# The routed part of a second FFN, computed for all tokens by every expert or for sorted blocks of 128 pairs

## The chip, the core and the metric

One Trainium2 chip, one of its cores. The program is written engine by engine: TensorE (PE, matrix products and transposes into PSUM), VectorE (DVE), ScalarE (ACT), GpSimd (POOL) and SyncE (SP, which issues the transfers), each with its own list of instructions, tied together by semaphores. The metric is the time of one execution in microseconds, the median of several. PSUM has 8 banks of 128 x 512 floats.

## The reference, cut to what matters

All is float32; 4 batches of 256 tokens, width 256, so 1024 tokens, computed in two halves of 512.

```python
x = x + ssm(ctx, layernorm(x))      # scan over 256 steps, 256 channels, 16 states
    # delta = softplus(dt_proj_w @ dt_lo + dt_proj_b);  state = state*exp(delta*A) + delta*u*B
x = x + ffn0(layernorm(x))          # 32 experts of 96 hidden units, top 8
x = x + cross_attention(layernorm(x), ctx)   # 16 heads of 128, 8 key heads
x = x + ffn1(layernorm(x)):
    shared   = silu(x @ wg_s) * (x @ wu_s) @ wd_s * 0.1          # 256 hidden units
    affinity = sigmoid(x @ centroids.T)                          # 16 experts
    top_idx  = top_k(affinity + gate_bias, 2)
    weights  = affinity[top_idx] / (sum of the two + 1e-9)
    for e in range(16):                                          # 128 hidden units each
        routed = routed + mask[:, e] * (silu(x @ wg[e]) * (x @ wu[e]) @ wd[e])
    return shared + routed
```

Each token uses 2 of the 16 experts; for the others its weight is zero.

## The kernel before, in words

A **half** is 512 tokens, 4 chunks of 128. Stages follow each other: the scan of half 0 (DVE: `scan_state` and `scan_read`, one pair for each of 16 states), the scan of half 1 interleaved with the first units of FFN 0, the rest of FFN 0, attention (64 head units, one for each half, head and batch), and FFN 1.

A **unit** of an FFN is 128 hidden units of weights times one half. `gate_up(u)` makes x @ gate and x @ up into two banks, ACT applies Silu (`activate_gate`), DVE multiplies by the up side and by the row of routing weights (`multiply_hidden`), and `down(u - 2)` adds the product with the down weights into two banks that hold the sum over all experts. Every unit multiplies all 512 tokens of its half, whether they chose the expert or not, and tokens of no weight are multiplied by zero. FFN 1 has 36 units: 2 of shared weights and 16 experts, for each half.

Nearly all products are made as **three products of a split** (`product3`): each operand is stored as a rounded high part and a rest, and hi x hi, hi x rest and rest x hi are added in PSUM. A unit is thus 12 + 6 = 18 instructions of 512 columns. The splitting costs too: ACT rounds each weight piece (`round_weights`), POOL subtracts (`rest_weights`), and the hidden values go through ACT and DVE (`round_hidden`, `rest_hidden`). The first 12 units of FFN 0 work on whole float32 operands instead (`gate_up_whole`, `down_whole`), where one product is recorded as two matmul instructions.

The order is written out by hand: each engine's list has loops over units or head units, and the steps between stages are numbered `transition(k, step)`: k = 6 and 7 lead from attention to FFN 1 for half 0 and 1, k = 8 and 9 from FFN 1 to the output. Steps 0 to 3 copy and turn the sum, add it to `x_tok` and find the variance, 4 normalises, 5 and 6 turn x for the products, 7 and 8 make the router's logits, 9 and 10 pick the two experts (`rank_experts`, `choose_two`, a row of small dependent DVE instructions), 11 turns the weights into rows. SP loads weights with `fetch`, broadcasts routing rows from a scratch in DRAM with `load_routes`, and stores the output pair by pair (`store_out`). An engine's list is executed in order: an instruction that waits holds up all behind it.

POOL's part in attention is `normalise(i)` for each head unit: it scales the probabilities by their inverse sums, and PE turns them two head units later (`turn_probs`, line 695). In the scan of half 0, ACT makes delta as Softplus with a bias (`activate_delta`), the decays as Exp (`scan_decay`), and the gate z (`normalise_z`, `activate_z`); the fold of the attention weights (`fold_turn`, `fold_multiply`) is laid between the scan's steps on PE and ACT.

## Time and profile before

| what | value |
|---|---|
| median of 3 runs | 744.71 us (744.0 to 747.23) |
| profiled execution, its own time | 747.59 us |
| profiled execution, span from first to last instruction | 745.9 us |
| PE busy | 682.9 us, 92% |
| DVE, ACT, POOL busy | 68%, 57%, 38% |
| mean granted clock of TensorE | 0.973 of full |
| moved by DMA | 88.1 MB |

By the timeline the stages are: scan of half 0 to about 90 us, scan of half 1 beside FFN 0 to 195 us, the rest of FFN 0 to about 354 us, attention to about 583 us, FFN 1 to the end. A busy share of PE is a sum over matrix products whose recorded durations overlap; the cost of one in a row of many is read from the distance between starts.

### The profile page before, as it was taken

How to read it: one execution, taken by the hardware profiler on the slowest of the kernel's cores; microseconds unless marked ns; L12 is line 12 of the kernel's file. 1: busy time of each engine (PE TensorE's matmuls, PEld its weight loads, DVE VectorE, ACT ScalarE, POOL GpSimd, SP SyncE). 2: the span in 40 equal slices, each digit the busy share in tenths (PEclk: the TensorE clock that was granted, in tenths of full speed). 3: DMA queues.
4: the chain of work that ended last, by engine and by line, in shares of the span. 5: the costliest groups of instructions: out<-in, count | busy, mean ns of one | idle time of the engine just before them, and what ended most of it. 6: DMA issues, size and time to landing. Idle time of an engine off the chain costs nothing.

```text
span 745.9 us, 10129 instructions
## 1 busy us (share of the span) xinstructions
PE 682.9 (92%) x3450; PEld 531.9 (71%) x3450; DVE 504.8 (68%) x990; ACT 423.7 (57%) x835; POOL 286.8 (38%) x266
## 2 busy tenths in 40 slices
PE   6476679999989999999899999997999899999997
PEld 1164445555767888887789999876997777888885
DVE  5789999999656655564766667766665566545444
ACT  5776746462265455454777777676876454343442
POOL 1456410002333334453555646444656243122131
PEclk9589987999999999999999999999999999999999
DMA  7359945676442644442110101100121235333240
GB/s 243 132 189 286 326 150 168 209 206 162 126 148 89 184 130 154 145 156 67 53 34 29 57 30 43 44 29 15 59 65 57 86 127 168 103 108 107 89 127 28
DMA packets 43666, 88.14 MB, mean 118 GB/s; under 512 B 6072, under 2 KB 8384, under 8 KB 43616
## 3 DMA queue, kind: packets, MB, share of 16 engines
q1 hardware_dynamic: 43616, 87.51, 37.5%
q8 instruction: 27, 0.44, 0.2%
q14 instruction: 23, 0.19, 0.1%
HBM read 81.92 MB, written 5.57 MB: 117 GB/s over the span
## 4 chain that ended last, share of the span: by engine, by line
PE 72%; DVE 13%; ACT 10%; issue 3%; POOL 0%; DMA 0%; SPq 0%; DVEq 0%; ACTq 0%
PE bank L91 19%; PE bank L92 19%; PE bank L93 19%; PE bank L503 5%; DVE state L1178 4%; PE bank L514 3%; PE bank L695 3%; ACT probs L1053 2%; ACT bank L813 2%; PE bank L422 2%; DVE scores L1459 1%; DVE head_out_lo L1103 1%; PE bank L410 1%; DVE x_tok L1202 1%; ACT head_out_hi L778 1%
## 5 line engine op out<-in xcount | busy, mean ns | idle before, releaser
L1532 POOL TENSOR_TENSOR w_lo<-w_raw,w_hi 128x768 fp32r<-128x768 f32 (+1 forms) x94 | 156.8, 1668 | 287.9 <-ACT w_hi L778 286.7
L91 PE MATMUL bank<-xt_hi,w_hi 128*128 128x512 f32 x352 | 140.7, 400 | 1.3 <-DVE hidden_lo L1103 1.3
L93 PE MATMUL bank<-xt_hi,w_lo 128*128 128x512 f32 x352 | 139.5, 396 | 0.0
L92 PE MATMUL bank<-xt_lo,w_hi 128*128 128x512 f32 x352 | 138.9, 395 | 0.0
L778 ACT ACTIVATE w_hi<-w_raw 128x768 fp32r<-128x768 f32 (+1 forms) x94 | 72.4, 770 | 103.0 <-PE bank L93 91.7
L1103 DVE TENSOR_TENSOR hidden_lo<-bank,hidden_hi 128x512 fp32r<-128x512 f32 x72 | 49.6, 690 | 67.6 <-ACT hidden_hi L778 67.6
L1342 DVE TENSOR_TENSOR bank<-gated,bank 128x512 f32<-128x512 f32 x68 | 47.2, 694 | 56.1 <-PE bank L93 52.7
L1053 ACT ACTIVATE probs<-scores,row_min 128x256 f32<-128x256 f32 x128 | 63.9, 501 | 25.7 <-DVE row_min L1459 25.5
L91 PEld LDWEIGHTS bank<-xt_hi,w_hi 128*128 128x128 f32 x352 | 66.2, 188 | 16.2 <-DVE hidden_lo L1103 2.1
L93 PEld LDWEIGHTS bank<-xt_hi,w_lo 128*128 128x128 f32 x352 | 66.1, 188 | 15.9
L921 ACT ACTIVATE gated<-bank 128x512 f32<-128x512 f32 x84 | 50.2, 597 | 46.0 <-PE bank L503 30.2
L92 PEld LDWEIGHTS bank<-xt_lo,w_hi 128*128 128x128 f32 x352 | 66.1, 188 | 13.7
L778 ACT ACTIVATE hidden_hi<-bank 128x512 fp32r<-128x512 f32 x72 | 42.5, 590 | 51.6 <-DVE bank L1345 50.1
L1603 POOL TENSOR_TENSOR probs<-probs,row_scale 128x512 f32<-128x512 f32 x64 | 66.7, 1042 | 5.0
L1459 DVE CUSTOM_DVE_ANT_0 scores<-bank,mask_bias 128x256 f32<-128x256 f32 x128 | 48.8, 418 | 13.8 <-PE bank L93 13.7
L91 PE MATMUL bank<-hidden_hi,w_hi 128*128 128x512 f32 x144 | 56.9, 395 | 0.8 <-DVE hidden_lo L1103 0.8
L92 PE MATMUL bank<-hidden_lo,w_hi 128*128 128x512 f32 x144 | 57.1, 396 | 0.0
L93 PE MATMUL bank<-hidden_hi,w_lo 128*128 128x512 f32 x144 | 56.1, 390 | 0.0
L1103 DVE TENSOR_TENSOR probs_t_lo<-bank,probs_t_hi 128x512 fp32r<-128x512 f32 x64 | 44.1, 688 | 15.4 <-ACT probs_t_hi L778 15.3
L778 ACT ACTIVATE probs_t_hi<-bank 128x512 fp32r<-128x512 f32 x64 | 38.2, 596 | 28.5 <-PE bank L695 28.1
L422 PEld LDWEIGHTS bank<-identity,read_out 128*128 128x128 f32 x272 | 31.9, 146 | 30.6 <-DVE read_out L1188 20.5
L422 PE MATMUL bank<-identity,read_out 128*128 128x128 f32 x272 | 37.2, 284 | 14.4 <-DVE read_out L1188 14.4
(173 smaller groups left out, 1451.0 us busy)
## 6 DMA issues: line engine op xcount, KB each, us to landing
w_raw<-in_ffn_w SPq DMA_DIRECT2D x62, 384.0 KB, 3.2
b_rows<-bc_scratch SPq DMA_DIRECT2D x32, 256.0 KB, 4.4
c_rows<-bc_scratch SPq DMA_DIRECT2D x32, 256.0 KB, 3.7
w_raw<-fold_scratch SPq DMA_DIRECT2D x32, 256.0 KB, 2.6
route_bc<-route_scratch SPq DMA_DIRECT2D x32, 256.0 KB, 3.6
route_bc<-route_scratch SPq DMA_DIRECT2D x31, 192.0 KB, 3.4
w_whole<-in_ffn_w SPq DMA_DIRECT2D x12, 384.0 KB, 4.8
fold_scratch<-fold_sb SPq DMA_DIRECT2D x8, 512.0 KB, 4.8
```

Source lines behind the costliest of these rows:

```text
L91: e.matmul(out, w_hi, m_hi, start=first, stop=False)
L92: e.matmul(out, w_hi, m_lo, start=False, stop=False)
L93: return e.matmul(out, w_lo, m_hi, start=False, stop=last)
L422: last = e.matmul(ps[:, l * DI + c * P:l * DI + (c + 1) * P], tile[:, c, t:t + P], identity[:, :], is_transpose=True, start=n < 0 and l + ...
L778: e.activation(out, source, ACT.Copy).then_inc(sem(name), 1)
L921: e.activation(gated[u % 2][:, :], bank[4 + 2 * (u % 2)][:, :], ACT.Silu).then_inc(sem("silu"), 1)
L1053: last = e.activation(probs[i % 3][:, r, :], scores_sb[i % 2][:, r, :], ACT.Exp, scale=-1.0, bias=row_min[i % 2][:, r:r + 1], accum_out=ro ...
L1103: e.tensor_tensor(out_lo, source, out_hi.bitcast(F32), ALU.subtract).then_inc(sem(name), 1)
L1342: e.tensor_tensor(h, g, h, ALU.mult).then_inc(sem("mul"), 1)
L1459: e.tensor_tensor_reduce(scores_sb[i % 2][:, r, :], bank[4 + i % 2][:, r * SEQ:(r + 1) * SEQ], mask_bias[:, half * HB + b, :], -SCALE, 3.0 ...
L1532: e.tensor_tensor(lo[:, 0:n], w_raw[(p - WHOLE) % RAW][:, 0:n], hi[:, 0:n].bitcast(F32), ALU.subtract).then_inc(sem("w_lo"), 1)
L1603: e.tensor_tensor(probs[i % 3][:, :, :], probs[i % 3][:, :, :], row_scale[i % 3][:, :].unsqueeze(2).broadcast_to([P, 2, SEQ]), ALU.mult).t ...
```

## The change

FFN 1's 32 routed units are replaced. `units1` keeps the 4 shared units (2 chunks for each half). The 1024 pairs of token and expert of a half are sorted by expert into blocks of 128 slots: at most 8 + 15 = 23 blocks for each half, since each expert rounds up, so 46 in all, worked through in 24 **rounds** of two blocks (the last round of a half has one). The number of blocks is fixed; slots that no pair fills hold zeros.

- **Sorting.** `choose_two` also writes `sel` (1 where a token chose an expert). PE counts earlier choosers with a triangular matrix (`count_earlier`, 8 small products in the place of `turn_route`); DVE turns counts into a slot for each pair (`count_blocks`, `find_slots`, step 12) and an expert for each block (`find_expert_of`) and the weights by pair (`find_weights`, step 13).
- **Moving.** SP writes zeros to the slot arrays in DRAM (`clear_slots`, 46 blocks of 128 KB). POOL scatters the normalised tokens, 8 indirect transfers of 128 rows for each half (`scatter_x`): those of half 0 in head unit 49 of attention, those of half 1 in FFN 1. SP loads a round's two blocks (`load_slots`) and stores its results (`store_slots`). POOL gathers the results back, again 8 indirect transfers for each half (`gather_outs`), and DVE adds them with the weight as scalar (`add_routed`).
- **Computing a round.** PE turns the slots (`turn_slots`), ACT copies them, PE makes gate and up of a block in one product of 256 columns, Silu and product follow at width 128, PE turns the hidden values (`turn_hid`), DVE copies them, PE makes the down product (`down_slots`), DVE copies the result to SBUF (`keep_slots`). All in whole float32, without split. The 16 experts' weights (6.3 MB) are loaded during attention and stay in SBUF; the PE operand is addressed by a register that `value_load` fills with the block's expert.
- **Order.** The shared units of half 0 become U0 and U0 + 1 of half 0, then the 24 rounds, and the two shared units of half 1 stand after the last `gate_up_slots`.
- **Start of the kernel.** Softplus becomes Exp, Ln(1 + .) on ACT and, on DVE, min(., 60) followed by max with the argument; the bias comes into PSUM by a product of one row (`bias_dt`). Exp of the scan shares the table with Ln. Half 1's delta, the skip, the z gate and the folds (from step 4, twice at steps 7, 10, 13) stand later in the lists. Several semaphores are merged (`ld_late`, `ld_proj`, `shift`).

```diff
--- before
+++ after
+LOG_CAP = 60.0
+BLOCKS = HT * TOP1 // P + E1 - 1
+PAIRS = (BLOCKS + 1) // 2
+ROUNDS = HALVES * PAIRS
...
-units1 = [(c, 0) for c in range(ALONE)]
+units1 = [(c, h) for h in range(HALVES) for c in range(SHARED_CHUNKS)]
...
-FOLD_FROM, FOLD_STEPS = 2, 2 * KV_HEADS
+FOLD_FROM, FOLD_STEPS = 4, 2 * KV_HEADS
+FOLD_TWICE = (7, 10, 13)
...
 def project_dt(h):
-    at.wait_ge("ld_dt_proj", 16)
+    at.wait_ge("ld_proj", 64)
     at.wait_ge("x_dbl_sb", h + 1)
     for c in range(EH):
-        ps = take(dt_bank(h, c), ("delta", 2 * h + c + 1))
+        ps = bank[dt_bank(h, c)]
         e.matmul(ps[:, :], dt_proj_sb[:, c * P:(c + 1) * P], x_dbl[0:DR, h * HT:(h + 1) * HT],
-                 start=True, stop=True).then_inc(sem("dt"), 1)
+                 start=False, stop=True).then_inc(sem("dt"), 1)
+def bias_dt(h, c):
+    at.wait_ge("ld_proj", 64)
+    at.wait_ge("consts", 4)
+    ps = take(dt_bank(h, c), ("delta", 2 * h + c + 1))
+    e.matmul(ps[:, :], dt_row[0:1, c * P:(c + 1) * P],
+             ones[0:1, :].unsqueeze(1).broadcast_to([1, HC, P]), start=True, stop=False)
...
-turn_z(0)
-turn_z(1)
-for n in range(-1, FOLD_FROM):
+for n in range(-1, DS):
     y_sum(0, n)
+    if n == 1:
+        turn_z(0)
+        turn_z(1)
+    for k in folds_at.get(n, ()):
+        fold(k)
...
+def find_experts(r):
+    h, pair = half_and_pair(r)
+    at.wait_ge("expert_of", h + 1)
+    for j in range(blocks_in(r)):
+        expert[r, j] = e.value_load(expert_of[h][0:1, 2 * pair + j:2 * pair + j + 1],
+                                    min_val=0, max_val=E1 - 1)
+def turn_slots(r):
+    n = blocks_in(r)
+    at.wait_ge(f"ld_slots{r % 3}", 16 * (r // 3 + 1))
+    ps = take(6, ("slots_t", r + 1))
+    for j in range(n):
+        for w in range(WH):
+            last = e.transpose(ps[:, (w * 2 + j) * P:(w * 2 + j + 1) * P],
+                               slots_in[r % 3][:, j, w * P:(w + 1) * P], identity[:, :])
+    last.then_inc(sem("slots_turn"), 1)
+def gate_up_slots(r):
+    at.wait_ge("ld_experts", 16 * E1)
+    at.wait_ge("slots_t", r + 1)
+    ps = take(4 + r % 2, ("slots_hid", r + 1))
+    for j in range(blocks_in(r)):
+        for w in range(WH):
+            last = e.matmul(ps[:, j * WIDTH:(j + 1) * WIDTH].rearrange("p (k i) -> p k i", k=2),
+                            slots_t[r % 2][:, w, j * P:(j + 1) * P],
+                            experts[:, bass.ds(expert[r, j] * 3, 2), w * P:(w + 1) * P],
+                            start=w == 0, stop=w == WH - 1)
+    last.then_inc(sem("slots_gate_up"), 1)
+def turn_hid(r):
+    at.wait_ge("slots_hid", r + 1)
+    ps = take(7, ("hid_t", r + 1))
+    for j in range(blocks_in(r)):
+        last = e.transpose(ps[:, j * P:(j + 1) * P], slots_hid[r % 2][:, j, :], identity[:, :])
+    last.then_inc(sem("hid_turn"), 1)
+def down_slots(r):
+    at.wait_ge("hid_t", r + 1)
+    ps = take(2 + r % 2, ("slots_out", r + 1))
+    for j in range(blocks_in(r)):
+        last = e.matmul(ps[:, j * WIDTH:(j + 1) * WIDTH], hid_t[r % 2][:, j * P:(j + 1) * P],
+                        experts[:, bass.ds(expert[r, j] * 3 + 2, 1), :].rearrange("p a n -> p (a n)"),
+                        start=True, stop=True)
+    last.then_inc(sem("slots_down"), 1)
...
+gate_up(U0 + 1)
+transition(7, 1)
+down(U0)
+transition(7, 2)
+find_experts(0)
+turn_slots(0)
+down(U0 + 1)
+for r in range(ROUNDS + 2):
+    find_experts(r + 1)
+    turn_slots(r + 1)
+    if r < ROUNDS:
+        gate_up_slots(r)
+    turn_hid(r - 1)
+    if r == ROUNDS:
+        gate_up(U0 + 2)
+    if r == ROUNDS + 1:
+        gate_up(U0 + 3)
+    down_slots(r - 2)
+    if r == 1:
         transition(7, 5)
         transition(7, 6)
+    if r in (2, 3):
+        transition(7, r + 5)
+    if r == 5:
         transition(7, 11)
+    if r in (6, 7):
+        transition(8, r - 5)
+down(U0 + 2)
+down(U0 + 3)
...
-        e.activation(delta[:, h, c, :], bank[dt_bank(h, c)][:, :], ACT.Softplus,
-                     bias=dt_bias[:, c:c + 1]).then_inc(sem("delta"), 1)
+        e.activation(delta[:, h, c, :], bank[dt_bank(h, c)][:, :], ACT.Exp).then_inc(sem("dt_exp"), 1)
+        at.wait_ge("dt_exp", 2 * h + c + 1)
+        e.activation(delta[:, h, c, :], delta[:, h, c, :], ACT.Ln, bias=1.0).then_inc(sem("dt_log"), 1)
...
-e.preload_act_table_set("softplus")
+e.preload_act_table_set("natural_log_exp_and_others")
+activate_delta(0)
 move_x_dbl(1)
-activate_delta(0)
-activate_delta(1)
-e.preload_act_table_set("exp_and_others")
 for n in range(2):
     scan_decay(0, n)
+activate_delta(1)
+make_skip(0)
 normalise_z(0)
-normalise_z(1)
 for n in range(DS):
     if n + 2 < DS:
         scan_decay(0, n + 2)
     if n == 0:
-        make_skip(0)
-    if n == 1:
+        normalise_z(1)
+    if n == 2:
         activate_z()
         e.preload_act_table_set("exp_and_others")
...
+def copy_slots(r):
...
+    copy(slots_t[r % 2][:, :, 0:n], bank[6][:, :].rearrange("p (w s) -> p w s", w=WH)[:, :, 0:n], "slots_t")
...
 def make_delta_u(h):
+    for c in range(EH):
+        at.wait_ge("dt_log", 2 * h + c + 1)
+        e.scalar_tensor_tensor(out=delta[:, h, c, :], in0=delta[:, h, c, :], scalar=LOG_CAP,
+                               in1=bank[dt_bank(h, c)][:, :], op0=ALU.min,
+                               op1=ALU.max).then_inc(sem("delta"), 1)
     for c in range(EH):
...
+def multiply_slots(r):
+    n = blocks_in(r)
+    at.wait_ge("slots_silu", r + 1)
+    at.wait_ge("hid_turn", r - 1)
+    e.tensor_tensor(slots_hid[r % 2][:, 0:n, :], slots_gate[r % 2][:, 0:n, :],
+                    bank[4 + r % 2][:, :].rearrange("p (j k i) -> p j k i", j=2, k=2)[:, 0:n, 1, :],
+                    ALU.mult).then_inc(sem("slots_hid"), 1)
+def copy_hid(r):
+    n = blocks_in(r) * P
+    at.wait_ge("hid_turn", r + 1)
+    at.wait_ge("slots_down", r - 1)
+    e.tensor_copy(hid_t[r % 2][:, 0:n], bank[7][:, 0:n]).then_inc(sem("hid_t"), 1)
+def keep_slots(r):
+    n = blocks_in(r)
+    at.wait_ge("slots_down", r + 1)
+    at.wait_ge(f"outs_stored{r % 3}", 16 * (r // 3))
+    e.tensor_copy(slots_out[r % 3][:, 0:n, :].rearrange("p j w -> p (j w)"),
+                  bank[2 + r % 2][:, 0:n * WIDTH]).then_inc(sem("slots_out"), 1)
+def add_routed(h):
+    for m in range(TOP1):
+        at.wait_ge(f"back{m}", 16 * HC * (h + 1))
+        for j in range(HC):
+            i = m * HC + j
+            if m > 0:
+                at.wait_ge("routed", h * HC * TOP1 + j + 1)
+            e.scalar_tensor_tensor(out=x_tok[:, h * HC + j, :], in0=back[i][:, :],
+                                   scalar=weight_of[h][:, m, j:j + 1], in1=x_tok[:, h * HC + j, :],
+                                   op0=ALU.mult, op1=ALU.add).then_inc(sem("routed"), 1)
...
+multiply_hidden(U0)
+add_acc(7, 0)
+rest_hidden(U0)
+multiply_hidden(U0 + 1)
+add_acc(7, 1)
+rest_hidden(U0 + 1)
+find_variance(half_of(7))
+for r in range(ROUNDS + 2):
+    multiply_slots(r)
+    copy_hid(r - 1)
+    if r == 0:
+        transition(8, 0)
+        transition(7, 4)
+    keep_slots(r - 2)
+    if r == 1:
         transition(7, 5)
         transition(7, 6)
+    if r == 4:
         transition(7, 9)
         transition(7, 10)
+    if r == 5:
+        transition(7, 12)
+    if r in (6, 7):
+        transition(8, r - 5)
+    if r == 8:
+        transition(7, 13)
+    if r == PAIRS + 7:
+        add_routed(0)
+    if r >= ROUNDS:
+        multiply_hidden(U0 + 2 + r - ROUNDS)
+        rest_hidden(U0 + 2 + r - ROUNDS)
+transition(9, 0)
+transition(9, 1)
+transition(9, 2)
+add_routed(1)
...
+def scatter_x(h):
+    at.wait_ge("x_norm", 5 + h)
+    at.wait_ge("slot_of", h + 1)
+    at.wait_ge("cleared", 16 * HALVES)
+    for m in range(TOP1):
+        for j in range(HC):
+            e.indirect_dma_start(
+                slots_dram[h], bass.IndirectOffsetOnAxis(slot_of_token[h][:, m, j:j + 1], 0),
+                x_norm[:, j, :], None).then_inc(sem(f"scattered{h}"), 16)
+def gather_outs(h):
+    for i in range(3):
+        at.wait_ge(f"outs_stored{i}", 16 * (((h + 1) * PAIRS - i + 2) // 3))
+    at.wait_ge("routed", h * HC * TOP1)
+    for m in range(TOP1):
+        for j in range(HC):
+            e.indirect_dma_start(
+                back[m * HC + j][:, :], None, outs_dram[h],
+                bass.IndirectOffsetOnAxis(slot_of_token[h][:, m, j:j + 1], 0)
+            ).then_inc(sem(f"back{m}"), 16)
...
+    if i == HEAD_UNITS // 2 + 17:
+        scatter_x(0)
...
+scale_norm(1, 8)
+scatter_x(1)
+gather_outs(0)
+gather_outs(1)
...
+def clear_slots(h):
+    at.wait_ge("sort_consts", 1)
+    e.dma_start(slots_dram[h].rearrange("(b p) w -> p b w", p=P),
+                nothing[:, :].unsqueeze(1).broadcast_to([P, BLOCKS, WIDTH])).then_inc(sem("cleared"), 16)
...
+def load_slots(r):
+    at.wait_ge("out", HEADS * HALVES)
+    at.wait_ge(f"scattered{r // PAIRS}", 16 * TOP1 * HC)
+    at.wait_ge("slots_turn", r - 2)
+    load(slots_in[r % 3][:, 0:blocks_in(r), :], rows_of(slots_dram, r), f"ld_slots{r % 3}")
+def store_slots(r):
+    at.wait_ge("slots_out", r + 1)
+    e.dma_start(rows_of(outs_dram, r),
+                slots_out[r % 3][:, 0:blocks_in(r), :]).then_inc(sem(f"outs_stored{r % 3}"), 16)
...
+    if i == 2:
+        clear_slots(0)
+    if i == 6:
+        clear_slots(1)
+    if i in EXPERT_LOADS:
+        load_expert(EXPERT_LOADS[i])
...
+for r in range(3):
+    load_slots(r)
+for r in range(ROUNDS + 2):
+    store_slots(r - 2)
+    load_slots(r + 3)
```

**PE in FFN 1.** Before, the last 9 of a step's 18 products, which repeat for every unit:

```order
L91 MATMUL bank<-xt_hi_76,w_hi 128x512
L92 MATMUL bank<-xt_lo_78,w_hi 128x512
L93 MATMUL bank<-xt_hi_76,w_lo 128x512
L91 MATMUL bank<-hidden_hi,w_hi 128x512
L92 MATMUL bank<-hidden_lo,w_hi 128x512
L93 MATMUL bank<-hidden_hi,w_lo 128x512
L91 MATMUL bank<-hidden_hi,w_hi 128x512
L92 MATMUL bank<-hidden_lo,w_hi 128x512
L93 MATMUL bank<-hidden_hi,w_lo 128x512
```

Now, PE in round 2: L842 is `find_experts` (a register load, and its bounds), L854 `turn_slots`, L865 `gate_up_slots` with a register instruction ahead of each product:

```order
L842 TENSOR_LOAD expert_of_210
L842 ISA x2
L842 TENSOR_LOAD expert_of_210
L842 ISA x2
L854 MATMUL bank<-identity,slots_in_212 128x128 x4
L865 ISA
L865 MATMUL bank<-experts,slots_t_215 128x256
L865 ISA
L865 MATMUL bank<-experts,slots_t_215 128x256
L865 ISA
L865 MATMUL bank<-experts,slots_t_215 128x256
L865 ISA
```

The round goes on with the fourth such product, two transposes (L877) and two down products (L886). The three-part products of 512 columns are gone from PE; register loads stand ahead of each round's first transpose.

**SP in FFN 1.** Before, in the part where both halves are worked through, weights and routing rows only:

```order
L1630 DMA route_bc_108<-route_scratch_0 128x512
L1630 DMA route_bc_109<-route_scratch_0 128x512
L1630 DMA w_raw_90<-in_ffn_w 128x768
L1630 DMA route_bc_110<-route_scratch_0 128x512
L1630 DMA w_raw_88<-in_ffn_w 128x768
L1630 DMA route_bc_107<-route_scratch_0 128x512
```

Now, from the last two loads ahead of the first store on:

```order
L1984 DMA slots_in_212<-slots_scratch 128x2x256
L1984 DMA slots_in_213<-slots_scratch 128x2x256
L2150 DMA outs_scratch<-slots_out_223 128x2x256
L1984 DMA slots_in_214<-slots_scratch 128x2x256
L2150 DMA outs_scratch<-slots_out_224 128x2x256
L1984 DMA slots_in_212<-slots_scratch 128x2x256
L2150 DMA outs_scratch<-slots_out_225 128x2x256
L1984 DMA slots_in_213<-slots_scratch 128x2x256
```

From round 2 on each load of a later round stands behind the store of an earlier one.

**POOL in attention**, head units 49 to 51. Before:

```order
L1600 TENSOR_TENSOR row_scale_181<-row_scale_181,any_valid 128x2
L1603 TENSOR_TENSOR probs_175<-probs_175,row_scale_181 128x512
L1600 TENSOR_TENSOR row_scale_182<-row_scale_182,any_valid 128x2
L1603 TENSOR_TENSOR probs_176<-probs_176,row_scale_182 128x512
L1600 TENSOR_TENSOR row_scale_180<-row_scale_180,any_valid 128x2
L1603 TENSOR_TENSOR probs_174<-probs_174,row_scale_180 128x512
```

Now:

```order
L1953 TENSOR_TENSOR row_scale_175<-row_scale_175,any_valid 128x2
L1956 TENSOR_TENSOR probs_169<-probs_169,row_scale_175 128x512
L1916 DMA slots_scratch<-x_norm,slot_of_token_203 2944x256 x8
L1953 TENSOR_TENSOR row_scale_176<-row_scale_176,any_valid 128x2
L1956 TENSOR_TENSOR probs_170<-probs_170,row_scale_176 128x512
L1953 TENSOR_TENSOR row_scale_174<-row_scale_174,any_valid 128x2
L1956 TENSOR_TENSOR probs_168<-probs_168,row_scale_174 128x512
```

The 8 scatters of half 0 stand between two `normalise` steps.

## Rows read from the trace of the kernel before

**Rows 1.** Busy time by stage: length, engines, granted clock, DMA share, GB/s.

```profile
core 0: us, PE busy (x) PEld busy (x) DVE busy (x) ACT busy (x) POOL busy (x), PEclk, DMA share, GB/s
26.00:45.00 19.00, 7.36 (x41) 6.62 (x42) 16.23 (x13) 17.88 (x29) 9.54 (x5) 0.55 0.31 101
45.00:90.00 45.00, 30.57 (x222) 24.38 (x221) 44.59 (x25) 30.71 (x56) 28.20 (x12) 1.00 0.87 285
468.00:582.00 114.00, 106.75 (x708) 94.61 (x707) 75.41 (x242) 80.41 (x208) 58.70 (x76) 1.00 0.16 50
590.00:735.00 145.00, 144.24 (x632) 115.38 (x631) 79.27 (x136) 61.46 (x97) 41.73 (x23) 1.00 0.36 111
```

**Rows 2.** Timeline of the passage from attention to FFN 1, PE and DVE.

```profile
584.33 0.40 PE L93 MATMUL bank<-head_out_hi,w_lo 128*128 128x512 f32 x1
...
584.77 0.69 DVE L1296 COPY acc_sb<-bank 128x512 f32<-128x512 f32 x1 [1.75 <-PE bank L93]
587.31 0.70 DVE L1347 SCALAR_TENSOR_TENSOR bank<-gated,bank 128x512 f32<-128x512 f32 x1 [1.85 <-ACT gated L921]
587.91 0.68 DVE L1202 TENSOR_TENSOR x_tok<-x_tok,bank 128x512 f32<-128x512 f32 x1
588.62 0.75 DVE L1121 BATCH_NORM_STATS2 stats<-x_tok 128x6 f32<-128x256 f32 x2
```

**Rows 3.** Transfers: size, us to landing; then the issues of `x_tok` by ns.

```profile
w_raw<-fold_scratch SPq DMA_DIRECT2D x32, 256.0 KB, 2.6
b_rows<-bc_scratch SPq DMA_DIRECT2D x32, 256.0 KB, 4.4
out<-x_tok SPq DMA_DIRECT2D x4, 256.0 KB, 2.2
route_scratch<-route_t SPq DMA_DIRECT2D x2, 64.0 KB, 1.6
...
L1707 SPq DMA_DIRECT2D out<-x_tok x4: 388/389/389, 712.3 to 743.3; - x4
```

**Rows 4.** Chain of waits, last pieces: start, duration, what.

```profile
741.15 0.64 PE bank L445 x4
741.80 0.02 issue
741.82 0.70 DVE x_tok L1202
742.54 0.69 DVE x_tok L1202
```

**Rows 5.** PE timeline where whole float32 products stand: start, duration, line, count.

```profile
123.04 1.04 PE L422 MATMUL bank<-identity,read_out 128*128 128x128 f32 x8
123.91 3.60 PE L503 MATMUL bank<-xt_whole,w_whole 128*128 128x512 f32 x8
127.35 1.88 PE L514 MATMUL bank<-hidden_whole,w_whole 128*128 128x512 f32 x4
```

**Rows 6.** Groups by line: 256-column operations of ACT and DVE.

```profile
L1053 ACT ACTIVATE probs<-scores,row_min 128x256 f32<-128x256 f32 x128 | 63.9, 501 | 25.7 <-DVE row_min L1459 25.5
L1459 DVE CUSTOM_DVE_ANT_0 scores<-bank,mask_bias 128x256 f32<-128x256 f32 x128 | 48.8, 418 | 13.8 <-PE bank L93 13.7
```

**Rows 7.** DVE timeline, dependent small operations of `choose_two`.

```profile
617.01 0.23 DVE L1274 SCALAR_TENSOR_TENSOR route_w<-route_a,logits 128x64 f32<-128x64 f32 x1
617.27 0.22 DVE L1277 TENSOR_REDUCE route_sum<-route_w 128x4 f32<-128x64 f32 x1
...
617.94 0.22 DVE L1283 TENSOR_TENSOR route_w<-route_w,route_sum 128x64 f32<-128x64 f32 x1
```

**Rows 8.** Timeline of the scan's start: ACT, then DVE.

```profile
23.73 0.69 ACT L797 ACTIVATE delta<-bank,small_sb 128x512 f32<-128x512 f32 x1 [1.01 <-PE bank L410]
...
26.14 1.28 ACT L962 ACT_TABLE_LOAD   x1
...
32.23 2.28 DVE L1178 TENSOR_TENSOR_SCAN state<-bank,drive 128x1024 f32<-128x1024 f32 x1
...
43.48 1.22 DVE L1188 TENSOR_TENSOR read_out<-state,c_rows 128x1024 f32<-128x1024 f32 x1 [1.75 <-PE bank L422]
```

**Rows 9.** Instructions by tile: ns min/median/max; last, POOL's timeline.

```profile
L1524 POOL TENSOR_TENSOR rstd<-rstd,half_power x8: 1007/1012/1922, 18.6 to 596.5; 128x4 f32<-128x4 f32 x8
L1136 DVE TENSOR_SCALAR x_norm<-x_tok,mean_var,rstd x8: 404/408/1997, 97.0 to 598.9; 128x256 f32<-128x256 f32 x8
...
598.88 1.85 POOL L1532 TENSOR_TENSOR w_lo<-w_raw,w_hi 128x768 fp32r<-128x768 f32 x1 [1.37 <-ACT w_hi L778]
```

**Rows 10.** Timeline of a head unit, POOL and the PE transposes that use it.

```profile
523.61 0.20 POOL L1600 TENSOR_TENSOR row_scale<-row_scale,any_valid 128x2 f32<-128x2 f32 x1 [2.89 <-DVE row_scale L1451]
523.88 1.04 POOL L1603 TENSOR_TENSOR probs<-probs,row_scale 128x512 f32<-128x512 f32 x1
...
526.56 0.60 PE L695 MATMUL bank<-identity,probs 128*128 128x128 f32 x4
```

414 lines of the change are left out of this document (277 added, 137 removed).

## Prediction

> **What bounds the kernel now.** I read the busy time by stage first [rows 1]. From 590 to 735 us PE is busy for 144.24 of 145 us at full clock, and in that stage the chain of waits runs almost wholly through products; DVE (79 us), ACT (61) and POOL (42) have room. So FFN 1 is bound by PE's count of instructions. The 632 products of the stretch give 145 / 632 = 0.229 us for each, so a unit of 18 costs 4.13 us, and 36 units 149 us. The last product of attention ends at about 584.6 us [rows 2], the span at 745.9, so what the change replaces is 161.3 us. Its end is short: four transposes at 741.15, two additions, and the store's 2.2 us to landing [rows 3, 4]. The profiled execution took 747.6 us, 2.9 above the median of 744.7; I sum differences against its span and apply them to both.
>
> **The price of a round on PE.** Whole float32 products show next to the scan [rows 5]: 4 products of 512 columns (x8 in the row, two records each) from 123.91 to 127.35 are 0.86 us each, so 0.43 at 256 columns, if time goes with columns. Eight transposes from 123.04 to 123.91 are 0.109 each. A round has 4 gate-and-up products, 2 down products and 6 transposes: 6 x 0.43 + 6 x 0.109 = 3.23 us. Over 46 blocks that is 74 us, where the 32 routed units took 132.
>
> **What else a round waits for.** Take the first slot transpose as zero: transposes to 0.43, gate and up to 2.15, hidden transposes to 2.37, down to 3.23. Silu of 256 columns takes 0.5 and the multiplication 0.42 [rows 6], so they end at 3.3; DVE then copies the hidden values (0.42, 3.7) and the result (0.69 as the 512-column copy in [rows 2], 4.4). Only then can SP store, 0.39 of issue, and behind it issue the load of round r + 3, another 0.39 [rows 3]: 5.2. A load of 256 KB lands 2.6 us after issue from `fold_scratch`, and 4.4 for `b_rows` in a crowded queue [rows 3]. Here a store of 256 KB stands ahead of it and its rows are 1 KB, so I take 3.1, near the first, since 512 KB in 4 us is 130 GB/s, where [rows 1] show 285 moved at full DMA load. That makes 8.3 us for a load that the first transpose needs two rounds later: a period of 4.15 us (3.9 with 2.6, 4.8 with 4.4, and never under 3.23). What is late in a round is thus the load behind the store, not PE.
>
> **FFN 1 after, term by term, from 584.6.**
> - Opening. `gate_up(U0 + 1)` 2.75 us. DVE must turn over `add_acc(7, 0)` before `rest_hidden(U0)`: 587.4 plus 0.4 of transposes, 0.68 + 0.75 + 0.69 [rows 2] and passing on, so `down(U0)` at 590.2; the same again holds `down(U0 + 1)` until 594.5. Rounds begin at 595.9: 11.3 us.
> - Rounds. The first two 3.5 each, 19 at 4.15, the last three, whose data are there, 3.4: 96.
> - In the rounds, half 1's router. A small dependent DVE step takes 0.25 us from start to start (617.01, 617.27) [rows 7]: sorting and slots are 11 such (2.8 us), experts and weights 13 (3.4), picking as before 3.1. DVE is free 2.6 us of each round, so only the excess shows, 0.2 to 0.8 each, but slots wait for PE's counts first: 1.5. Two ACT table loads at 1.28 [rows 8] put the next Silu back by 1.2. PE's own extras (transposes 0.9, logits 1.4, counts 1.3, sums 0.9) are half covered by its wait: 2.3. In all 7.5.
> - The two shared units behind the rounds and the products among them: 7.0. They are the cover of nothing but the last stores.
> - End. Result copy and store 3.2; then POOL gathers: no row shows an indirect transfer. It is at least SP's 0.39 for a plain issue and, unless it waits for landing, hardly over POOL's longest power of 4 columns, 1.92 us; the median of those, 1.01 [rows 9], is the nearest thing to a fixed price on POOL, and 128 addresses come on top: I take 1.3. Eight are 10.4, landing 2.2, addition 0.7, output 2.6: 18.9. PE's last products and the acc path (about 6 us) are hidden beside these.
> Sum 11.3 + 96 + 7.5 + 7.0 + 18.9 = 140.7, against 161.3: **-20.6 us**.
>
> **Attention.** The 8 scatters of half 0 stand on POOL between two head units. A unit has 2.9 us of idle time ahead of POOL's step, and its result is used 1.6 us after it ends (524.92 to 526.56) [rows 10]; of the idle 2.9 some 1.0 is given to a weight rest in other units, so 3.5 of 10.4 us are covered and turn_probs waits 6.9. What is queued behind them is `normalise`, on which PE waits. DVE's steps 12 and 13 (2.8 and 3.4 us) stand in two units in a row where DVE has 1.05 free of 3.3 (75.4 busy of 114 [rows 1]): 4.1. PE counts 1.0. Clearing writes 6 MB in SP's queue ahead of weight loads that are two pieces early: 1, with 0 to 10 as bounds; the 6.3 MB of experts come at 60 GB/s and cost nothing while the load stays under the 285 of [rows 1]. Together **+13**.
>
> **The start.** Before, ACT's Softplus of half 1 starts at 23.73, behind PE, and state 1 of the scan at 32.23; later DVE loses 1.75 us at 43.48 to the z transposes on PE [rows 8]. After, half 0 runs earlier, but DVE stops in step 1 for half 1's delta, which needs two more one-row products at half clock (0.55 in [rows 1]), a second function and a maximum: state 1 at about 33, and no stop at 43. One table load less is off the path. **-1**, between -4 and +4. The scan itself stays at DVE's pace.
>
> Net: -20.6 + 13 - 1 = -8.6 us: 739 for the profiled execution, **736** against the median, -1.2%.
>
> **Two rules of the Trainium skill.** The first speaks against the gathers and scatters. Rows: one x_norm operation on DVE took 1997 ns where the median is 408, starting at 598.9, just as a POOL subtraction of 1.85 us began at 598.88 [rows 9]; so the two do hold each other up. The Trainium skill (SBUF — State Buffer, section "SBUF: two separate sides") says that a DVE operation in a two-port mode keeps GpSimd from writing descriptors of its transfers. By that rule each of the 8 could wait for 0.4 of DVE work, +3 at the end; nearly all DVE work in the rounds has a PSUM operand, and I leave the sum as it is. The second: the Trainium skill (DMA: Bandwidth & Descriptors, section "Latency and other measured facts") gives 0.6 us as the floor of a tensor_load. Two in a round would be 1.2, an estimate by that page of +0.3 a round, 7 us in all; the trace of before has no register load.
>
> **The rivals.**
> 1. *Register loads on PE become the bound* (slower). No row prices them. From below they are hidden: PE's list waits 0.9 us a round for the load anyway, so up to 0.45 each is free. From above, a round trip to memory is the 1.6 us that 64 KB take to land [rows 3]. At 1.0 each, the middle, a round is 3.23 + 2.0 = 5.2 us, 22 x 1.1 = +24: 760. It decides from 0.45 us a load. For it: they stand ahead of each round's transposes, in order. Against: products of the round before may still be queued. 14%.
> 2. *Indirect transfers run one after the other* (slower). If POOL can't prepare one until the last has landed, each is 1.0 + 2.2 = 3.2 us, not 1.3; 16 on the path (8 scatters, 8 gathers) add 30: 766. 11%.
> 3. *The clock falls.* Between 26 and 45 us PE is busy 39% and has 0.55 of the clock, which is the level of 1.2 GHz; between 45 and 90 us at 68% it has 1.00 [rows 1]. Rounds are busy 78%. If they fell, 3.23 would be 6.5: +2.3 x 24 = 55, 791. 5%.
> 4. *The loads aren't late.* Round at 3.4, transfers at 1.0 each: -14 - 5: 717. 20%.
> 5. The forecast, period 3.7 to 4.6 and 1.0 to 1.7 for each indirect transfer: 722 to 749, 50%.
>
> **Numbers.** About 0.5% (3.7 us) is what a measurement can tell from no change, so 741.0 and 748.4 are the borders. Of the forecast's 50, 38 lie below, 10 between, 2 above. Faster: 38 + 20 = 58. Same: 10 + 1 of rival 1 = 11. Slower: 2 + 13 + 11 + 5 = 31. The range leaves the clock case and the far ends of the others out: 713 to 766.
>
> **What would show it.** Right: starts of slot transposes 4.15 us apart with PE waiting for slots_in; a gap of some 7 us on PE in head unit 52 behind the scatters; PE busy under 85% after 600 us at full clock; 8 gathers filling 10 us at the end. Wrong: gaps after TENSOR_LOAD with slots_in long landed (rival 1); scatters 3 us apart (rival 2); half clock (3); 3.3 between rounds (4); a scan that ends over 4 us away from 90 us.

## The result, and the profile after

| | before | after |
|---|---|---|
| median, us | 744.7 | 734.8 |
| lowest to highest | 743.6 to 747.2 | 729.1 to 736.7 |
| profiled execution, its span | 747.6, 745.9 | 729.07, 727.3 |
| ratio of the times, 95% interval | | 0.985 (0.981 to 0.988) |

The change makes the kernel 1.5% faster: 9.9 us by the medians, where 8.6 was forecast (736.0). The profiled execution of the changed kernel is the shortest of five, 18.5 us below that of before; the four others took 734.6 to 736.7. What sets it apart from them is what half of the experiments ask. One execution of e3_const took 1275 us, was slow as a whole, and is left out of every number below.

Busy time by stage of the changed kernel (columns as in [rows 1]): from the sorting of half 0 to the end of attention, the opening of FFN 1, the rounds, the end.

```profile
508.00:598.00 90.00, 74.34 (x462) 66.22 (x463) 55.24 (x180) 47.70 (x125) 44.81 (x56) 0.92 0.10 33
598.00:609.50 11.50, 7.62 (x39) 5.87 (x38) 6.50 (x16) 4.76 (x7) 1.01 (x1) 1.00 0.30 91
609.50:704.00 94.50, 85.07 (x460) 69.39 (x459) 45.48 (x131) 27.61 (x55) 15.55 (x17) 1.00 0.45 141
704.00:727.30 23.30, 8.34 (x39) 6.22 (x37) 9.11 (x17) 2.28 (x4) 7.83 (x8) 0.74 0.28 85
```

PE, busy for 144.24 of 145 us in FFN 1 before [rows 1], is so for 85 of 94.5 in the rounds. In the stretch of attention shown first it has 15.7 us without work and a mean clock of 0.92.

The scatters of half 0 on POOL (timeline), and the chain of waits behind them:

```profile
535.67 1.04 POOL L1956 TENSOR_TENSOR probs<-probs,row_scale 128x512 f32<-128x512 f32 x1
536.90 1.23 POOL L1916 DMA_INDIRECT slots_scratch<-x_norm,slot_of_token  x1 [0.19 <-issue]
...
546.03 0.96 POOL L1916 DMA_INDIRECT slots_scratch<-x_norm,slot_of_token  x1 [0.30 <-issue]
547.30 1.04 POOL L1956 TENSOR_TENSOR probs<-probs,row_scale 128x512 f32<-128x512 f32 x1
548.39 1.11 PE bank L779 x4
```

The probabilities before the scatters come at 535.67, the next at 547.30, 11.6 us later; before the change two such steps of POOL are 3.4 us apart in the mean (216.8 us for 63). PE's transposes of unit 50 wait for them for 6.9 us.

The chain in the rounds (start, duration, what):

```profile
653.62 0.66 PE bank L854 x4
654.27 0.86 PE bank L865 x4
655.14 0.22 PE bank L877 x2
655.36 0.88 PE bank L886 x4
...
656.26 0.70 DVE slots_out L1778
656.98 0.36 SPq L2150
...
657.38 3.28 DMA slots_in<-slots_scratch
...
660.71 0.39 PE bank L854 x2
```

From the transposes of one round the chain goes to a result copy, its store (0.36), the load behind it and the transposes two rounds on, 7.1 us later. This is the quiet part of the rounds: from 649 to 668 us two rounds take 7.1 to 7.4 us, but from 616.03 to 695.82 the 20 rounds take 4.0 each, since half 1's router, the transfers of half 1 and the additions stand among them. PE's list of waits from 612 to 700 us agrees: `L854 <- DMA slots_in` has 14 waits, 8.7 us in all, and nothing else has over 0.4.

The end, as the chain has it (`L886` is the last down product):

```profile
707.80 0.45 PE bank L886 x2
708.27 0.44 DVE slots_out L1778
708.72 1.70 DMA outs_scratch<-slots_out
...
711.24 0.95 POOL back L1927
...
718.75 1.21 POOL back L1927
...
720.26 2.74 DMA back<-outs_scratch,slot_of_token
```

### The profile page after: what moved, and what is told of

It is laid out like the page before. It is cut to its first block, busy times and chain, and to the rows that moved or that the text cites. A ratio compares the mean times of both kernels' runs of the same rounds, so it can differ in the third digit from the quotient of the medians.

```text
span 727.3 us, 10135 instructions
## 1 busy us (share of the span) xinstructions
PE 637.9 (88%) x3320; PEld 499.8 (69%) x3320; DVE 492.7 (68%) x1034; ACT 391.6 (54%) x798; POOL 276.0 (38%) x280
## 4 chain that ended last, share of the span: by engine, by line
PE 46%; DVE 27%; issue 8%; ACT 8%; DMA 5%; POOL 4%; SPq 1%; DVEq 0%; POOLq 0%; ACTq 0%
PE bank L96 13%; PE bank L97 12%; PE bank L98 12%; DVE state L1366 9%; DMA slots_in<-slots_scratch 3%; DVE read_out L1376 3%; PE bank L865 3%; ACT probs L1209 3%; PE bank L779 2%; DVE scores L1717 1%; DVE stats L1301 1%; DVE u_sb L1292 1%; DVE head_out_lo L1283 1%; POOL slots_scratch L1916 1%; PE bank L854 1%
## 5 line engine op out<-in xcount | busy, mean ns | idle before, releaser
L1847 POOL TENSOR_TENSOR w_lo<-w_raw,w_hi 128x768 fp32r<-128x768 f32 (+1 forms) x70 | 112.7, 1611 | 174.1 <-ACT w_hi L930 173.1
L96 PE MATMUL bank<-xt_hi,w_hi 128*128 128x512 f32 x224 | 90.2, 403 | 1.3 <-DVE hidden_lo L1283 1.3
L97 PE MATMUL bank<-xt_lo,w_hi 128*128 128x512 f32 x224 | 88.7, 396 | 0.0
L98 PE MATMUL bank<-xt_hi,w_lo 128*128 128x512 f32 x224 | 88.7, 396 | 0.0
L779 PE MATMUL bank<-identity,probs 128*128 128x128 f32 x256 | 39.2, 276 | 12.8 <-POOL probs L1956 8.0
L96 PEld LDWEIGHTS bank<-xt_hi,w_hi 128*128 128x128 f32 x224 | 42.4, 189 | 10.4 <-DVE hidden_lo L1283 2.1
L98 PEld LDWEIGHTS bank<-xt_hi,w_lo 128*128 128x128 f32 x224 | 42.2, 188 | 10.2
L1881 POOL TENSOR_TENSOR drive<-delta_u,b_rows 128x1024 f32<-128x1024 f32 x16 | 38.6, 2415 | 27.9 <-DVE read_out L1376 18.8
L96 PE MATMUL bank<-probs_t_hi,ctx_tok_hi 128*128 128x256 f32 x128 | 42.0, 328 | 6.9 <-DVE head_out_lo L1283 6.9
L565 PE MATMUL bank<-xt_whole,w_whole 128*128 128x512 f32 x96 | 43.9, 601 | 0.0
```

Of the source, the lines that this page charges most:

```text
L96: e.matmul(out, w_hi, m_hi, start=first, stop=False)
L97: e.matmul(out, w_hi, m_lo, start=False, stop=False)
L98: return e.matmul(out, w_lo, m_hi, start=False, stop=last)
L779: last = e.transpose(ps[:, s * SEQ + r * P:s * SEQ + (r + 1) * P], probs[i % 3][:, r, s * P:(s + 1) * P], identity[:, :])
L1847: e.tensor_tensor(lo[:, 0:n], w_raw[(p - WHOLE) % RAW][:, 0:n], hi[:, 0:n].bitcast(F32), ALU.subtract).then_inc(sem("w_lo"), 1)
```

## Experiments

A total says little here, since executions of one kernel differ by several us. Attention and the end agree far better between profiles in which nothing of them was changed: attention took 232.6 to 232.7 us in five of them, 232.1 in the changed kernel's own, and the end 15.7 to 16.1. The rounds do not: their column differs by 3 us and more for reasons that are not the edit. So the verdicts on attention and the end rest on this table, those on the rounds on the table and the chains, in us: start of the first probabilities; from there to the last; from the first slot turn to the first gather of half 1 (rounds); from there to the end; span and median. The 17.6 us between the last probabilities and the first slot turn (19.0 in e1_spread, 19.1 in e11_thin) have no column. Each row is one profiled execution, and its median is of 3 to 10 executions. The constant experts of e3_const, the fixed rows of e7_plain and the thin rows of e11_thin make another output, so these three only measure.

| kernel | first prob. | attention | rounds | end | span | median |
|---|---|---|---|---|---|---|
| before | 357.6 | 216.8 | | | 745.9 | 744.7 |
| after | 355.9 | 232.1 | 105.6 | 16.1 | 727.3 | 734.8 |
| e1_spread | 357.7 | 225.0 | 115.1 | 16.1 | 732.9 | 734.6 |
| e2_ahead5 | 359.0 | 232.7 | 102.3 | 15.9 | 727.6 | 729.1 |
| e3_const | 358.9 | 232.7 | 108.5 | 16.0 | 733.8 | 735.8 |
| e5_tail | 360.3 | 232.6 | 109.3 | 15.9 | 735.7 | 736.4 |
| e6_paced | 359.0 | 232.6 | 118.5 | 16.1 | 743.8 | 741.6 |
| e7_plain | 358.6 | 225.1 | 111.8 | 10.7 | 723.9 | 724.8 |
| e8_front | 360.0 | 223.6 | 117.7 | 16.0 | 735.0 | 735.5 |
| e9_all | 359.8 | 223.5 | 103.2 | 16.0 | 720.1 | 721.7 |
| e10_best | 355.5 | 223.7 | 98.6 | 15.9 | 711.3 | 717.1 |
| e11_thin | 358.9 | 232.7 | 116.3 | 15.7 | 742.7 | 743.9 |
| e12_spaced | 358.9 | 223.5 | 106.5 | 15.8 | 722.4 | 723.2 |
| e13_both | 360.0 | 223.5 | 105.1 | 15.9 | 722.1 | 722.9 |

**The scatters of half 0, spread.**

```diff
-if i == HEAD_UNITS // 2 + 17:
-    scatter_x(0)
+if 0 <= i - HEAD_UNITS // 2 - 17 < TOP1 * HC:
+    scatter_x(0, [i - HEAD_UNITS // 2 - 17])
```

> The eight scatters of half 0 are issued one in each of head units 49 to 56 and no longer all in unit 49. My theory: POOL has 2.9 us of idle time ahead of its step in each unit, so one transfer of 1.25 us fits beside it; PE's wait for the probabilities of unit 50 (6.9 us, with 0.8 around it) goes, attention ends 7 to 8 us earlier, total 726 to 728 against 734.8. Rival: POOL's step is already what the next products wait for in most units; then each transfer delays its unit by 0.5 to 1.25 us and the wait is only cut in pieces: 0 to -3 us.

Attention was 7.1 us shorter, as the theory had it, and the median the same (734.6; all four executions took 732.2 to 736.4, so the loss elsewhere is in each of them). The rounds took 9.5 us longer than in the changed kernel's profile. By the starts of the slot turns, 3.3 us of that are lost ahead of the first scatter of half 1, where a slot load lands 4.5 us after its issue (621.43) and finds PE waiting for it; 5.4 us at the stop that follows here; 0.8 later. Their chain at the stop:

```profile
640.62 0.59 DVE x_tok L1390
641.21 5.83 issue
...
647.11 0.28 DVE slots_hid L1760
```

5.83 us of "issue", waiting for nothing that the profile shows. The timeline (the last brackets: idle time before, releaser) has the first `L865` there, 8 records of a gate-and-up, from 640.87; ACT's Silu of it can start at about 642.8 and starts at 646.62:

```profile
640.87 1.89 PE L865 MATMUL bank<-experts,slots_t 128*128 x8
644.94 0.96 POOL L1916 DMA_INDIRECT slots_scratch<-x_norm,slot_of_token  x1 [0.30 <-issue]
646.62 0.38 ACT L1248 ACTIVATE slots_gate<-bank 128x256 f32<-128x256 f32 x1 [4.40 <-remote]
647.11 0.42 DVE L1760 TENSOR_TENSOR slots_hid<-slots_gate,bank 128x256 f32<-128x256 f32 x1 [5.90 <-issue]
```

So a result of PE was passed on 4 us late. The semaphore events in the trace show that all four signals of PE in that stretch (gate-and-up, hidden transposes, down, slot turn) come 2.4 to 4.4 us after their products by the record, close together from 646.60 to 647.45, behind POOL's last of eight scatters (644.94). Under the gathers of half 0 one more signal is 1.4 us late, at 682, and a slot load lands 4.7 us after its issue. The changed kernel's profile has no late signal, the only one of eleven profiles with indirect transfers in rows beside the rounds of which that is so. Whether that is its lead over the four other executions isn't shown, since their traces weren't kept.

The granted clock shows a second part. Behind some of PE's waits it stands at half, which is the level of 1.2 GHz. In this profile PE waited 2.0 us for the late slot load, and then (windows, granted clock 0.57):

```profile
626.00:630.00 4.00, 4.00 (x13) 3.34 (x14) 1.47 (x11) 0.60 (x1) 0.00 (x0) 0.57 0.40 118
```

Added up over the rounds, the clock stands at half for none of the time in the changed kernel and e2_ahead5, about 3 us in e3_const, 7 in e7_plain, 10 in e1_spread, e5_tail and e8_front, 14 in e11_thin and 17 in e6_paced. Among the profiles with three buffers the rounds column follows that order nearly (105.6, 108.5, 111.8, then 109.3 to 118.5, where e5_tail is shorter by 4.9 through its own edit). While PE works at half clock it loses half of the time: a late load or a late signal costs its own wait and this on top.

**Five slot buffers.**

```diff
-for r in range(3):
+for r in range(5):
     load_slots(r)
 for r in range(ROUNDS + 2):
     store_slots(r - 2)
-    load_slots(r + 3)
+    load_slots(r + 5)
```

> Five buffers for slots_in in the place of three: round r + 5 is loaded behind the store of round r - 2. My theory: the load behind the store sets the period (14 waits of PE for slots_in with 8.7 us in all, and 49% of the chain from 640 us on); with two rounds more to land they go, the rounds end 6 to 9 us earlier, total 726 to 729. Rival 1 (register loads or PE's own count of products): the waits get another name, 0 to -2 us. Rival 2: loads of half 1 stand in SP's queue ahead of stores and wait for its scatters until 648 us, which holds up stores of half 0: 0 to +4 us.

Faster by the rounds, 102.3 us in spite of two stops; the median is 5.7 us lower (ratio to before 0.981, 0.977 to 0.986), though the slowest of its four executions (733.5) lies among those of the changed kernel. PE no longer waits for `slots_in`. Between the stops a round now takes what PE takes; the chain has nothing but its products (here of round 11, which has one block and so one hidden transpose less):

```profile
661.63 0.44 PE bank L854 x4
662.07 1.73 PE bank L865 x8
663.80 0.11 PE bank L877
663.91 0.87 PE bank L886 x4
664.77 0.44 PE bank L854 x4
```

The load behind the store was the bound, and the price of a full round on PE is 3.25 us (slot turns at 667.43, 670.68, 673.93 and 677.18).

**No register loads.**

```diff
-expert[r, j] = e.value_load(expert_of[h][0:1, 2 * pair + j:2 * pair + j + 1],
-                            min_val=0, max_val=E1 - 1)
+expert[r, j] = (2 * pair + j) % E1
```

> No register loads: the expert of each block is a fixed number, so the routed part of the output is another one; products, transposes and transfers are the same in number and size. My theory: register loads stand in PE's list while PE waits for slots_in anyway, 0 to -1.5 us. Rival: at 0.45 us a load or more they hold up every round, and without them the rounds are over 0.3 us shorter each: -7 us or more.

735.8, no gain. Ahead of all stops, from the first slot turn to the ninth, it is 0.7 us shorter than the changed kernel (30.7 against 31.4), under 0.1 a round. The rival is out; the rounds of 3.25 us above have two register loads in each.

**The shared units of half 1 behind the last down product.**

```diff
-if r == ROUNDS:
-    gate_up(U0 + 2)
-if r == ROUNDS + 1:
-    gate_up(U0 + 3)
 down_slots(r - 2)
+if r == ROUNDS + 1:
+    gate_up(U0 + 2)
+    gate_up(U0 + 3)
```

> The two shared units of half 1 stand behind the last down product of the rounds on PE, DVE and ACT, in the place of between the last turns of hidden values and the last down products. My theory: two times 2.8 us of shared products stand ahead of the last two down products; without them the last store is issued about 4.5 us earlier and with it the eight gathers and the end: -4 to -5 us, 730. Rival: the products of the shared units, their acc path and additions (12 us behind the rounds) then end later than the gathers and take the place: -1 to -2 us.

From the issue of the fourth last store of results to the first gather it is 6.6 us (713.29 to 719.85) where it was 11.4 (699.82 to 711.24), and the end is no longer: the 4.9 us were there. The median (736.4, of 733.1 to 739.0) doesn't show them. The profile has a stop under the scatters, late slot loads under the gathers and 10 us at half clock (rounds 109.3, which without the edit would be 114.2); why its four executions all have so much isn't known.

**Paced transfers.** POOL waits for the slot turn of rounds 7 to 10, then 16 to 19, before each pair of transfers.

```diff
-scatter_x(1)
+for pair in range(TOP1 * HC // 2):
+    at.wait_ge("slots_turn", 7 + pair)
+    scatter_x(1, [2 * pair, 2 * pair + 1])
...
+if h == 0:
+    at.wait_ge("slots_turn", 16 + (m * HC + j) // 2)
```

> The scatters of half 1 and the gathers of half 0 go out two in each round (POOL waits for the turn of rounds 7 to 10, then 16 to 19) and no longer eight in a row; the additions of half 0 and its stores stand two rounds later. My theory: while POOL issues indirect transfers in a row, instruction fetches and slot loads are held up; that gives the rounds of 6 to 8.6 us between stores 5 and 6 and between stores 13 and 14 which the profiles of all four variants have and the one of the changed kernel has not. Paced, no distance between stores is over 5.5 us and the median falls to 728 to 731. Rival: one indirect transfer is enough to hold a fetch for 4 us, then the long rounds stay or spread, 733 to 737. Second rival: slots of half 1 come later, PE waits at round 12 for over 3 us.

Worse, 741.6, and for the scatters no test: PE's turns run ahead so far that the waits were met, and all eight went out 1.3 us apart, only 7 us later. The stop came with them, one round later. The gathers did go out apart: four in a row, then two at 687.51 and two at 693.27. No signal of PE is late under them. But a slot load landed 4.5 us after its issue at 681.55, and the products behind it ran at half clock (0.50 from 686 to 692), which makes 9.2 us between two stores.

**Plain transfers.**

```diff
-e.indirect_dma_start(slots_dram[h], bass.IndirectOffsetOnAxis(slot_of_token[h][:, m, j:j + 1], 0),
-                     x_norm[:, j, :], None)
+e.dma_start(slots_dram[h][(m * HC + j) * P:(m * HC + j + 1) * P, :], x_norm[:, j, :])
```

and the gathers likewise.

> The 32 indirect transfers are plain ones of the same size from the same place on POOL, with fixed rows in the place of sorted ones, so the routed part of the output is another one. My theory (it is the row-by-row, POOL-made form of the transfers that holds others up, and costs POOL 1.25 us each): a plain issue takes POOL under 0.6 us, the gap in head unit 50 shrinks from 6.9 to under 1 us, the 10 us of gathers at the end shrink to under 5, and the long rounds go: 710 to 716. Rival (traffic as such): the gap and the tail shrink as well, but rounds of 6 us and more stay between stores 5 and 6 and between 13 and 14: 717 to 722.

Eight plain issues take POOL 4.4 us and not 10:

```profile
632.35 4.37 POOL L1916 DMA_DIRECT2D slots_scratch<-x_norm  x8 [27.12 <-DVE slot_of_token L1509]
```

The gap in attention went as in e1_spread, and the end is 5.4 us shorter. No signal of PE is late in this profile. But one distance between stores (13 to 14) is still 9.1 us: ACT waits there 5.3 us for slot transposes that wait for a slot load beside 1 MB of gathers, and the products behind it run at half clock, 3.39 us where they take 1.74:

```profile
667.94 5.67 DMA slots_in<-slots_scratch
...
673.66 0.66 PE bank L854 x4
674.32 3.39 PE bank L865 x8
```

So there are two effects under the gathers: slot loads land late beside either kind of transfer, and PE's signals are late beside indirect ones alone. The total, 724.8, lies above both forecasts, since the rounds (111.8) kept the first; late slot loads with three buffers and the half clock behind them are enough for long rounds without any late signal.

**Sorting in pieces, scatters spread, folds moved.**

```diff
-FOLD_TWICE = (7, 10, 13)
+FOLD_TWICE = (4, 6, 13)
...
-if step == 12:
-    count_blocks(k)
-    find_slots(k)
-if step == 13:
-    find_expert_of(k)
-    find_weights(k)
+if step == 12:
+    count_blocks(k)
+if step == 13:
+    finish_places(k)
+    find_slots(k)
+if step in (14, 15, 16):
+    find_expert_of(k, [8 * (step - 14)])
+if step in (17, 18):
+    find_weights(k, [step - 17])
```

> Three edits ahead of FFN 1: the scatters of half 0 one in each of 8 head units; slots, experts and weights of half 0 found in 7 pieces in 7 units and no longer in two units in a row; folds twice at steps 4, 6 and 13 so that the store of one fold and the load of another no longer stand together at step 12 of the scan. Theory: attention, which took 15.3 us longer than before between the first and the last probabilities (7.7 of it ahead of the scatters, 7.6 by them), takes 2 to 5 us longer; the late rows of B at step 14 (2.2 us of DVE) are gone. Both show in the trace. The median falls by 10 us less what rounds give back: 725 to 730. Rival on sorting: DVE's order of units, not the length of one stop, counts, and the pieces cost as much together: attention stays 7 us longer or more. Rival on the folds: that row load was late by chance, and another step of the scan loses the same 2 us.

(The half 0 form is shown, without its conditions on k.) Attention is 6.8 us longer than before, not 2 to 5: spreading the scatters gave 7.1, the pieces only 1.5 more. The rival on the pieces is right: most of the sorting costs the same in two units or in seven. The folds gave nothing either; POOL waited 5.1 us for rows of B in the changed kernel and 7.7 here. A late row load moved to another step.

**Everything, then the best.** e9_all has all edits above but constants and plain transfers (loads of half 1 not ahead of step 9).

> All edits together: those ahead of FFN 1, five buffers for slots_in (loads of half 1 not ahead of step 9), indirect transfers of the rounds two in each round, shared units of half 1 behind the last down product. If the gains are independent: 7 to 10 (attention), 2 (scan), 3 to 6 (rounds), 4.8 (end, as the distance from the last full store to the first gather showed), so 715 to 719. If what one gives another takes back, as the first four runs would have it when only totals are read: 725 to 735.

721.7 (ratio 0.969, 0.966 to 0.972), between the two forecasts: of the changes read by stage (8.6 in attention, 4.9 ahead of the last gathers, 5.7 by five buffers, 19 in all) 13 us come out, so most of the gains do add. Its chain shows two new costs near the end: additions of half 0 between the copies on which PE waits, and a store of output ahead of the last store of results.

```profile
690.68 0.45 DVE x_tok L1802 x2
691.38 1.00 DVE x_tok L1802 x3
692.57 1.27 DVE x_tok L1802 x3
...
698.77 4.54 DMA outs_scratch<-slots_out
```

```diff
-if r == PAIRS + 9:
-    add_routed(0)
+if 0 <= r - 20 < TOP1 * HC // 2:
+    add_routed(0, [r - 20])
...
-if r in (PAIRS + 11, PAIRS + 12):
-    store_out(8, r - PAIRS - 11)
+for k in (8, 9):
     for pair in range(HC // 2):
-        store_out(9, pair)
+        store_out(k, pair)
```

> All edits of the version with everything, but folds as in the changed kernel, scatters of half 1 in a row again, additions of half 0 two in each of rounds 20 to 23 in the place of eight in one round, and the four stores of output behind the last store of results. In that version's trace the eight additions stopped PE for 2.5 us, and a store of output ahead of the last store of results made it land after 4.5 us, where it lands after 1.7 in the changed kernel. Theory: -2.5 and -2.8, so 715 to 718. Rival: DVE's additions beside the copies of hidden values cost as much in four pieces, and POOL's start of the last gathers does not follow the store: 720 to 722.

(The lines taken out are those of e9_all; folds and scatters of half 1 are again as in the changed kernel.) 717.1 (713.0 to 719.0), 0.964 of before (0.961 to 0.968): the fastest of all, 17.7 us under the changed kernel, and as forecast. Its chain still has a stop under the scatters:

```profile
632.44 5.25 issue
```

**What in the indirect transfers stops PE.** First their bytes: rows of 16 columns in arrays of their own.

```diff
-slots_dram[h], bass.IndirectOffsetOnAxis(slot_of_token[h][:, m, j:j + 1], 0), x_norm[:, j, :], None
+thin_dram[h], bass.IndirectOffsetOnAxis(slot_of_token[h][:, m, j:j + 1], 0), x_norm[:, j, 0:16], None
```

> The changed kernel, but its 32 indirect transfers move 16 columns of each row (8 KB in the place of 128 KB) to and from arrays of their own, with the same sorted rows and the same 1.25 us on POOL; the routed part of the output is another one. In eight profiles PE's results are passed on up to 5 us late while a row of eight indirect transfers goes out, never with plain transfers of the same bytes. If it is the making of such transfers on POOL that holds them back, the late results stay: stores 5 to 6 or 13 to 14 over 6 us apart, a chain with pieces of issue over 3 us in rounds, 733 to 737. If it is the bytes, rows scattered one by one among slot loads and stores: no such pieces, distances of 5 us at most, 726 to 730.

With a sixteenth of the bytes both stops are there (PE's signals 1.3 to 4.8 us late near 653, 1.7 to 3.3 near 688), the distances between stores are 8.7, 8.1 and 9.0 us, and the total is 743.9, worse than I had for that case; 14 us of its rounds are at half clock. The chain, then the same products in the timeline:

```profile
650.13 2.77 PE bank L866 x8
...
652.92 0.39 ACT slots_gate L1249
```

```profile
649.96 1.89 PE L866 MATMUL bank<-experts,slots_t 128*128 x8
```

By their records the products of `L866` take as long as elsewhere and end at 651.85; the chain gives them 2.77, since it runs on to the late signal at 652.89. It isn't the bytes of the indirect transfers. Then the row: each transfer waits for the landing of the one ahead.

```diff
-scatter_x(1)
+for piece in range(TOP1 * HC):
+    at.wait_ge("scattered1", 16 * piece)
+    scatter_x(1, [piece])
```

> On the fastest version: each scatter of half 1 waits until the one ahead of it has landed, so they stand some 3.5 us apart and not 1.25 (8 take 28 us and not 10); loads of half 1 begin one step later. In the profiles so far results of PE are passed on up to 5 us late only under rows of eight, with thin rows as with full ones, and never in attention under single transfers, one in a unit. If it takes the row, the stop of 5.25 us of the chain under the scatters goes; half 1's slots then come at about 656, and the load that waits for them costs 0 to 3: 712 to 716. If one transfer in rounds is enough, the stop stays or comes more often: 717 or more.

> As the one before, and the gathers of half 0 wait for each other's landing in the same way; the additions of half 0 stand two rounds later. If the row is what stops PE, the second stop (PE's hidden transposes, 2.3 us at one place, and slot loads 2.5 us late) goes too, and the end is 1 us later for the additions: 709 to 714. If not: 715 or more.

In e12_spaced the scatters stand 2.7 to 3.6 us apart and no signal of PE is late under them. That is half a test: in the rows of eight the late signals come near the end, and here PE is without work beside the last scatters. Under the gathers, in a row but for one gap of 2.7 us, four are late (2.0 to 3.2 us, at 680). In e13_both none is late anywhere. Its gathers are the clean case, 3.0 to 4.1 us apart with PE at work beside all eight, and the chain under them is bare products:

```profile
675.72 0.44 PE bank L854 x4
676.16 1.73 PE bank L865 x8
677.89 0.22 PE bank L877 x2
678.11 0.87 PE bank L886 x4
678.97 0.44 PE bank L854 x4
```

So, of what was tried, signals are late only beside indirect transfers issued in a row, 1.25 us apart, and not even beside all of those: the changed kernel's profile has none, and e5_tail has none over 0.7 us under its gathers. Waiting for each landing also leaves only one in flight, and no run tells that from the distance.

What is held up stays open, and one rival is untested: the recording of the trace. Each of these transfers leaves 16 landing events where none is missing, 128 for eight. Under the scatters of half 1 the trace has 19 to 34 of the 128 in each of the nine profiles with late signals there, and all 128 in the four without (the changed kernel, e7_plain, e12_spaced, e13_both). Under the gathers of half 0 it has 22 to 58 in the eight profiles with signals over 1 us late, 47 in e5_tail, 107 in e6_paced, and all 128 in the changed kernel, e7_plain and e13_both. So where signals are late, other events are missing. Something may hold up both, or the writing of events may hold up the engines; no execution here is known to have gone unrecorded, so these runs can't tell, nor say how much of the stops is left without the profiler.

As a remedy the waits fail, for the slots of half 1 come at 653 to 654 and PE runs dry: two slot turns are 14.8 us apart where 3.25 are usual. First e12_spaced (windows, granted clock 0.74), then the load in the chain of e13_both:

```profile
640.00:656.00 16.00, 4.50 (x24) 3.42 (x23) 4.76 (x15) 1.15 (x3) 3.83 (x4) 0.74 0.34 117
```

```profile
654.19 2.66 DMA slots_in<-slots_scratch
```

723.2 and 722.9, 6 us slower than e10_best: the wait costs more than the stops. Both lie in the range that I had for the case that the row is not the cause; by the traces it is PE's wait for half 1's slots, which I had put at 0 to 3 us, that took them there.

## Why the prediction was right, point by point

The size came out right against the median, 734.8 for 736, and partly by luck. Against the profiled execution it was 10 us off (739 forecast, 729.1 measured), and there the parts can be compared: FFN 1 -32.2 us where -20.6 was forecast (129.1 from the last product of attention to the end, for 161.3), attention +15.3 for +13, the start -1.7 for -1.

- **Opening**, 11.3 forecast: the last product of attention ends at 598.2, the turn of round 1 starts at 609.5, 11.3.
- **Price of a round on PE**, 3.23 forecast: 3.25 in e2_ahead5 and e13_both.
- **The load behind the store as bound**, period 4.15: the mechanism is right, the size too high. Per term: transposes to issued load 4.6 us by the median of 19 rounds (4.5 from 656.58 to 661.10), not 5.2, since DVE starts the result copy 0.34 us behind the copy of hidden values where I had used whole durations; landing 3.0 by the median of 24, not 3.1. Two quiet rounds took 7.1 to 7.4, so 3.6 to 3.7 a round and not 4.15. PE waited for `slots_in` 8.7 us in all, where 19 waits of 0.9 make 17.
- **Rounds, router's extras and shared units** together 110.5. From the turn of round 1 to the last down product the profiled execution needs 98.8 (609.5 to 708.3), 11.7 less, all of it in the rounds and extras: 91.6 where 96 and 7.5 make 103.5. By an estimate from the quiet rounds, 19 times 0.5 is 9.5 of that. In the profiles with stops and three buffers it is 102 to 112 (the table's rounds column less 3.8 and 3.0). The forecast had no stops, no late slot loads and no half clock behind them: a too long period stood in for them, so the sum fitted the usual execution by luck. This is the step that was wrong.
- **DVE's experts and weights** of half 1 (3.4 forecast) stand in the chain from 645.51 to 648.92: 3.4, not the 0.2 to 0.8 of excess over its slack, since PE's next round needed DVE right then.
- **Shared units of half 1**, 7.0 on the path, "the cover of nothing": right, and e5_tail shows that they need not be there.
- **PE busy** under 85% after 600 us was named as a sign of being right. It was 87% up to 704 (90.69 of 104 us), by the shorter period.
- **End**, 18.9: result copy to span end 708.3 to 727.3, 19.0. Each gather 1.25, against 1.3; the longest landing 2.7, against 2.2.
- **Attention**, +13: +15.3 (232.1 against 216.8). Up to unit 46 the probabilities of both kernels keep a distance that is constant to 0.05 us, so the clearing and the loading of the experts cost 0, not 1. By unit 49 sorting has cost 7.6, against 5.1; the scatters add 7.7, against 6.9.
- **Start**, -1, between -4 and +4: the first probabilities are 1.7 us earlier than before in the profiled execution, but in eleven profiles with this start they come between 355.5 and 360.3 (middle 358.9, +1.3 against the one profile of before). State 1 of the scan starts at 32.6 (33 forecast). What varies is row loads; the chain has one of 7 us behind a fold's store and load:

```profile
65.11 2.27 POOL drive L1881
67.37 7.01 DMA b_rows<-bc_scratch
74.51 3.33 POOL drive L1881
77.91 2.30 DVE state L1366
```

The kernel was not run with the old start and the new FFN 1, so the start's share stays unproven.

**The rivals.** Register loads (1): out, e3_const. The Trainium skill (DMA: Bandwidth & Descriptors, "Latency and other measured facts") puts a floor of 0.6 us under a tensor_load, from which I had +0.3 a round; with two in each round of 3.25 us, the runs show less than 0.1 a round of it on the path. Serial transfers (2): out, the second scatter starts 1.3 us after the first. Falling clock (3): not as put, for it is 1.00 in the rounds of the changed kernel's profile; but it falls behind waits of PE, in attention (0.78 from 530 to 548) and in the rounds of most other profiles (3 to 17 us at half), and this small form of the rival had no place in the forecast. Loads not late (4): out for three buffers (PE waits 8.7 us for them), true with five. The forecast of half the chance (5), 722 to 749, held.

The other rule of the Trainium skill (SBUF — State Buffer, "SBUF: two separate sides"), by which two-port work of DVE holds up GpSimd's descriptors, would have put 3 us on the last gathers. They start 1.24 to 1.26 us apart beside DVE's additions of 713.9 to 715.3 (PSUM operand), and 1.5 apart only once, 718.75 to 720.26, where DVE adds gathered rows from SBUF: 0.25 us at most. So this trace shows next to nothing of such a loss. The stops in the rounds are another matter: there PE's signals are late beside POOL's transfers.

## What to carry to other kernels

Before a row of indirect transfers is put beside products, count two prices: POOL's 1.25 us each, and, at least when profiled, signals of PE up to 5 us late near the end of the row; spread them where one fits into POOL's idle time, and give the rounds a buffer or two more than the mean period asks for. Where a load's issue stands behind a store in the same queue, the length of the loop is what counts, and one more buffer in the ring cuts it. When a change mends one stage and the total doesn't move, compare stages, not totals, and then the granted clock: here -7.1 and -4.9 us were real, and in all four executions of each experiment longer rounds took them back, by late loads, late signals and half clock behind both. And when signals come late in a trace, count its events before trusting that the cause lies in the kernel.

## What the runs showed of the hardware

- An indirect transfer of 128 rows costs POOL 1.24 to 1.27 us from start to start behind the first of a row (0.95 busy), with rows of 1 KB and of 64 B alike; a plain one from the same queue 0.55 (eight in 4.37).
- Beside a row of eight of them PE's signals were up to 5 us late in rounds (10 of 11 such profiles, the longest 2.3 to 5.0 us in each), and landing events were missing from the trace in the same places; with ones 3.0 us or more apart and PE at work beside all eight there was neither (gathers of e13_both, one profile).
- Behind a wait of PE of 2.0 us (e1_spread, 626.00) and behind the late load of e7_plain (673.66) the granted clock was half, and eight products of a round took 3.3 to 3.4 us and not 1.74.
- A slot load of 256 KB landed 3.0 us after its issue by the median of the changed kernel, and 4.1 to 5.7 beside gathers (the changed kernel, e1_spread, e6_paced, e7_plain).
- Two register loads ahead of a round of 3.25 us on PE cost under 0.1 us a round (e3_const against the changed kernel over the first eight rounds).
- Small dependent steps of DVE start 0.25 us apart with 64 columns and 0.32 with 128 (647.41 to 648.94 and 645.42 to 647.32 in the changed kernel).
